# The load of every third group of m issued from ScalarE's queue in the second pass of a graph network kernel

## What is computed

```python
h = jnp.maximum(_layernorm(x, axis=-1), 0.0)
# of the layer, with x = h, row = src, col = dst, bcol = 0:
e = jnp.concatenate([h[row], bcol[row], edge_attr], axis=1)
e = relu(_bn(e @ W1 + b1, g1, be1))              # statistics over all edges
ssum = segment_sum(e, col, num_segments=12500)
agg = ssum / jnp.maximum(cnt, 1.0)[:, None]
h2 = jnp.concatenate([h, bcol, agg], axis=1)     # 385 columns
h2 = relu(_bn(h2 @ W2 + b2, g2, be2))            # statistics over all nodes
return x + relu(h2 @ W3 + b3)
```

## Time and profile before

| what | us |
|---|---|
| median of three runs (lowest, highest) | 3292.05 (3285.0, 3298.05) |
| the profiled execution | 3268.36 |
| its span | 3266.6 |
| PE busy in the span | 2494.8 (76%) |
| DVE busy | 1807.0 (55%) |
| GpSimd (POOL) busy | 1755.0 (54%) |
| ACT busy | 973.6 (30%) |
| clip of a group, L1007, 416 times | 492.9, mean 1213 ns |
| slot sums, L1337, 3322 matmul records | 261.6, mean 393 ns |

### The profile page before, as it was taken

One profiled execution on the slowest core, in us unless ns is written; L12 is line 12 of the kernel. 1 busy time (PEld: TensorE's weight loads), 2 busy tenths in 40 slices (PEclk: granted clock), 3 DMA queues, 4 the chain that ended last, 5 costly groups with the idle time before them and its releaser, 6 DMA issues.

```text
span 3266.6 us, 42293 instructions
## 1 busy us (share of the span) xinstructions
PE 2494.8 (76%) x14769; PEld 1082.0 (33%) x14769; DVE 1807.0 (55%) x5121; ACT 973.6 (30%) x1601; POOL 1755.0 (54%) x1847
## 2 busy tenths in 40 slices
PE   1467777774777777777777777777777899999998
PEld 1332332222323323323322232223232444444448
DVE  2444444455545444444444454444444899889878
ACT  1321221121222212221222121222212555565546
POOL 7246666666666666666666666666665222222220
PEclk7778877887777777777787788777787999999999
DMA  6356666665666666666666666566565999999965
GB/s 180 126 181 202 217 201 205 219 214 170 219 214 218 205 200 210 208 200 212 206 207 214 198 219 206 192 209 213 194 217 196 344 342 342 343 345 342 343 246 158
DMA packets 270664, 741.36 MB, mean 227 GB/s; under 512 B 46391, under 2 KB 98661, under 8 KB 270448
## 3 DMA queue, kind: packets, MB, share of 16 engines
q1 hardware_dynamic: 189152, 525.28, 44.9%
q0 software_dynamic: 78432, 212.46, 22.1%
q10 hardware_dynamic: 2864, 0.86, 0.1%
HBM read 501.63 MB, written 236.81 MB: 226 GB/s over the span
## 4 chain that ended last, share of the span: by engine, by line
PE 58%; issue 17%; another core or an unknown queue 7%; POOL 6%; DVE 5%; DMA 4%; ACT 1%; SPq 0%; DVEq 0%; POOLq 0%; ACTq 0%
PE psum L1224 16%; PE psum L1177 11%; PE psum L1318 6%; POOL sums L562 6%; PE psum L1337 6%; PE psum L1190 4%; DMA late<-m_d 3%; PE psum L1180 2%; PE psum L1179 2%; PE psum L1178 2%; PE psum L1348 2%; PE psum L1403 2%; DVE sums L966 1%; PE psum L1279 1%
## 5 line engine op out<-in xcount | busy, mean ns | idle before, releaser
L562 POOL DMA_INDIRECT sums<-P_d,late x1581 | 1504.0, 951 | 900.2 <-issue 452.5
L966 DVE TENSOR_TENSOR sums<-psum,sums 128x1024 f32<-128x1024 f32 x396 | 482.9, 1219 | 974.2 <-remote 826.6
L650 ACT ACTIVATE sums<-sums 128x1024 f32<-128x1024 f32 x416 | 438.6, 1055 | 1733.6 <-remote 1172.1
L1224 PE MATMUL psum<-late,sums 64*128 64x256 f32 x3320 | 707.9, 469 | 294.4 <-issue 241.1
L1224 PEld LDWEIGHTS psum<-late,sums 64*128 64x128 f32 x3320 | 384.2, 218 | 827.5 <-issue 705.8
L1177 PE MATMUL psum<-sums,ones 128*32 128x512 f32 x830 | 539.8, 730 | 70.6 <-issue 64.8
L1180 PE MATMUL psum<-sums,ones 128*32 128x512 f32 x830 | 537.8, 725 | 44.8 <-issue 42.5
L1178 PE MATMUL psum<-sums,ones 128*32 128x512 f32 x830 | 546.3, 738 | 29.8 <-issue 28.0
L1179 PE MATMUL psum<-sums,ones 128*32 128x512 f32 x830 | 541.3, 731 | 35.3 <-issue 33.7
L929 DVE TENSOR_SCALAR late<-late 128x98 bf16<-128x98 bf16 x1661 | 441.7, 278 | 178.3 <-remote 142.1
L1007 DVE TENSOR_TENSOR late<-late,psum 128x1024 f32<-128x1024 f32 x416 | 492.9, 1213 | 36.6 <-DMA late<-m_d 32.6
(11 more groups left out here) (187 smaller groups left out, 1985.1 us busy)
## 6 DMA issues: line engine op xcount, KB each, us to landing
m_d<-sums SPq DMA_DIRECT2D x415, 512.0 KB
late<-m_d SPq DMA_DIRECT2D x415, 512.0 KB, 5.4
sums<-in_ea_main SPq DMA_DIRECT2D x103, 512.0 KB
sums<-P_d,late POOLq DMA_INDIRECT x1581
P_d<-sums SPq DMA_DIRECT2D x24, 512.0 KB, 2.9
nodes<-in_x SPq DMA_DIRECT2D x24, 256.0 KB
late<-in_x SPq DMA_DIRECT2D x24, 256.0 KB, 3.3
out<-late SPq DMA_DIRECT2D x24, 256.0 KB, 2.5
```

The source lines that it names most:

```text
L562: pool.indirect_dma_start(out=m_s[s][0:r, k * L:(k + 1) * L], out_offset=None, in_=P1_d, in_offset=bass.IndirectOffsetOnAxis(ap=idx[0:r, G ...
L966: dve.tensor_tensor(m_s[s][0:r, 0:w], ps_m[place_m[g]][0:r, 0:w], m_s[s][0:r, 0:w], ALU.add).then_inc(s_m, 1)
L1224: ins = pe.matmul(ps_m[place_m[g]][:, k * L:(k + 1) * L], ea[lo:lo + EF, a:a + P], W1c[lo:lo + EF, :], start=True, stop=g not in xg_no, sk ...
```

## The change

In the second pass the loads of those groups g that are at least 6 and have g % 3 = 2 (8, 11, ..., 413: the last group of each set) are left out of SP's list and issued by ACT. ACT issues the load of group 3 (s + 2) + 2 right behind its copy of the slot sums of set s. That copy has waited for `s_l1` of 3 s + 3, which is what the load waits for on SP. Slot, size, source and landing semaphore are the same. All other loads stay on SP.

```diff
+        def on_second_queue(g):
+            return g >= M2_SLOTS and g % SG == SG - 1
+
+        assert M2_SLOTS == 2 * SG
...
             with sp.If_eq(flag, 0):
                 for g in range(NG):
+                    if on_second_queue(g):
+                        continue
                     if g >= M2_SLOTS:
                         sp.wait_ge(s_l1, g - M2_SLOTS + 1)
                     r, w = rows(g), tiles(g) * L
...
                         if s >= 2:
                             act.wait_ge(s_seg, s - 1)
                         act.activation(slot_s[:, s % 2, :], ps_slot[s % 2], ACT.Copy).then_inc(s_slot, 1)
+                        g = (s + 2) * SG + SG - 1
+                        if g < NG:
+                            act.dma_start(m2_s[g % M2_SLOTS][0:rows(g), 0:tiles(g) * L],
+                                          m_d[g, 0:rows(g), 0:tiles(g) * L]).then_inc(s_ml[g % M2_SLOTS], 16)
                 copy_odd()
```

## The result

The changed kernel takes 3302.31 us in the median of 20 runs (3291.45 to 3313.6), the kernel before 3291.57 us over 20 runs (3282.39 to 3299.82). The ratio is 1.0031, with a 95% interval of 1.002 to 1.0041: slower by about 10.7 us, and inside the half per cent that the prediction counted as no change. With 20 runs of each it can be told from zero all the same.

What follows compares the result with a forecast made beforehand. PE was taken to bound most of the second pass, the DMA engines only short stretches. Terms 0 + 0 + 0 + 3.6 gave +4 us, 3272 us profiled or 3296 us on the median's scale; range 3273 to 3330.

Steps and rivals of the forecast that it cites:

- The terms put at 0: Second pass: SP's saved issues, ACT's added issues and the later leaving of the moved load, each costed at 0.
- Two of the signs: If right, in the second pass: PE's waits for DVE near 23 us, and loads with g % 3 = 1 later.
- SP's time: SP's queue loses 136 issues of 0.33 us, 45 us; each leaves when PE frees a slot, so worth 0.
- ACT's time: ACT's queue: 136 issues, 58 to 154 us, fit its idle time; taken as 0, with 5 us for the range.
- The moved load's departure: Behind ACT's copy, the moved load leaves 0.04 to 0.39 us later, plus at most 0.8; costed at 0.
- The expectation that no load would gain PE anything: Second pass: PE is the bound in most stretches; earlier data could win at most 22.9 us; sum 0 and no less.
- Who shares the DMA engines: Second pass: two queues share the engines, so a moved load holds back the one needed before it; +3.6 us.
- 14 x 0.66 x 0.39: 14 loads without reserve, each costing the load before it half a load, 0.66 us; 0.39 reaches PE; +3.6 us.
- The slower rival: Stretches refilling behind a late load: moved load overtakes the one before it; 21 to 42 us, 3313 to 3334; chance 0.26.

Runs made afterwards that it cites:

- the last two runs: On another chip, against the kernel before: only the younger load of the 23 pairs on ACT's queue, ratio 1.0043; the changed kernel repeated, 1.0044.

## Why the prediction was right, and what in it was wrong

The forecast, no change by half a per cent with a lean of +4 us, held, and the time is in its range; the slowdown of 10.7 us lies on the side of the lean. The terms put at 0 were right for the reasons given. The one term that mattered was small enough to stay inside the half per cent, and that was partly luck: its place was wrong, and all of its three factors were too small. Two of the signs that the prediction named also failed: PE's waits in the pass were 35.5 us, not near 23, and the loads with g % 3 = 1 did not land later (a median of 5.43 us before, 5.32 after).

- SP's time, 0: right. Its issues waited for PE as before.
- ACT's time, 0 by the 0.43 us row: right. 0.33 us, beside the copy; the transfer in place of the load gave 0.9999.
- The moved load's departure, 0.04 to 0.39 us late, cost 0: right. It was 0.01 us, and 0.46 us on SP gave 0.9997.
- The expectation that no load would gain PE anything, since PE was full: right. Moved loads in calm stretches landed 0.14 us sooner (5.28 to 5.14 us) and the time did not fall.
- "Who shares the DMA engines", the step priced at +3.6 us: this is where all of the loss is, and the term was too small by three. That two queues share was right. Wrong was who pays. The prediction had the moved load hold back the one needed before it, at g % 3 = 1. The rows show no rise there (7.3 and 7.2 us), though 8 of 63 loads there now landed less than 0.7 us ahead of the moved load, none before: the older load of a pair pays to the younger one issued right behind it, and in this change the older one is the moved load itself. Each factor of 14 x 0.66 x 0.39 was low. The count was 23 pairs, the 15 and the 8 at the start of the pass, not 14. The lateness was half a load, 0.66 us, in the prediction; the older loads of the 23 pairs landed 22.0 us later in sum, 0.96 us each (the median of the 15 rose by 1.1). Of that 22.0 us, 10.5 came through to PE, 0.48 instead of 0.39: its waits before these loads rose from 0.7 to 11.2 us. 23 x 0.96 x 0.48 is 10.6 us. Between DVE and PE nearly all of it came through here: DVE's waits for these loads rose by 11.7 us, so at these places hardly any group stood clipped ahead. Why so little stood in reserve was not tested. The trace of before would have told the place: those issues stand 0.4 us apart in it.
- The slower rival named the right place, stretches that refill behind a late load, and priced 21 to 42 us; measured were 10.7. It needed 25 of 136 sets to lose 0.66 us of PE's time each; 23 pairs lose 0.46 us each on average (10.5 / 23).

The Trainium skill, page "DMA: Bandwidth & Descriptors", section "Queues, rings and completion order", has each DMA engine go round between the queues with work, packet by packet. The landings and the shares of q1 and q10 agree: two loads 0.42 us apart, 1.28 us between their landings on one queue, 0.2 to 0.5 us on two. The section "Issuing engines are not separate DMA queues" says that a second issuing engine saves issue time only; here that meant no gain, and the runs add that it may cost.

What stays open: why the first group of each such burst (g % 3 = 0) already lands about 1 us late in the kernel before, and how the loss with g % 3 = 1 moved divides exactly.

## What to carry to other kernels

On one queue the loads here landed in the order of issue, 1.3 us apart where they queued, and a consumer that takes loads in order wants just that: before a second queue is used, look for the places where two loads leave within a load's own time (1.3 us here), not at the average spacing. A load that is 1 us late at a few places costs PE about half of that where the reserve is used up (10.5 of 22.0 us), while a hundred loads elsewhere cost nothing. A split of the moved items by one property of the trace, one kernel for each part, shows the cause where a single on-off comparison of 0.3% can't.

## What was not expected of the hardware

The longest waits behind late loads were followed by a lower clock. In the changed kernel PE sat idle 1.93 us, and its granted clock in the 4 us from 2787 was 0.57, mostly the lower level of 1.2 GHz, then full again; the same around a wait of 2.56 us that began at 2997.

```profile
2785.93 0.64 PE L1347 MATMUL psum<-late 128*32 128x256 f32 x8 [1.93 <-DVE late L1017]
```

```profile
2780.00:2787.00 7.00, 4.49 (x40) 1.75 (x40) 5.09 (x7) 1.76 (x5) 0.37 (x2) 1.00 1.00 398
2787.00:2791.00 4.00, 4.00 (x20) 0.86 (x18) 3.69 (x5) 2.42 (x6) 0.51 (x1) 0.57 0.77 216
2791.00:2798.00 7.00, 7.00 (x61) 3.30 (x54) 5.43 (x8) 2.82 (x7) 0.83 (x1) 1.00 0.81 257
...
2999.00:3006.00 7.00, 6.17 (x24) 1.55 (x28) 5.73 (x6) 2.79 (x6) 0.83 (x1) 0.52 0.69 235
```

In the profile of before the clock never fell between 2600 and 3100 us. The loss does not need it, since the kernel with 23 moved loads has the loss and no such fall in that stretch of its profile; but where it comes, a wait costs more than its length. The length of a wait alone does not decide it: in the kernel with the loads of g % 3 = 1 moved the clock stayed full after one of 2.42 us, and in the one with only the 23 loads moved it fell after one of 1.74 us near the start of the pass.

SP's issue of the younger load took 1.30 us instead of 0.33 in the burst shown above, with the loads before it outstanding; after the change none of SP's issues took over 0.6 us. It changed nothing, as the younger load landed no sooner.

The chip of the last two runs did the kernel before in 2849.31 us, 442 us less than the first, and yet the second pass took almost the same: in the changed kernel 654 us from the first slot sums to the last (2107.8 to 2761.8), and 657 on the first chip (2545.2 to 3202.5). The difference is in the first pass, behind which the first load leaves at 2098.8 us instead of 2537.8. The ratio of the change was the same within the intervals.
